# A one-core decoder layer: the lower-left block of the delta rule's inverse moves from the values to the scores

## The reference

```
def gated_delta_rule(q, k, v, g, beta):          # q, k, v: 32 x 128 x 8 heads x 128
    def step(S, inp):                            # S: heads x 128 x 128, one step per position
        qt, kt, vt, gt, bt = inp
        S = S * exp(gt)
        kv = einsum('bhk,bhkv->bhv', kt, S)
        delta = (vt - kv) * bt
        S = S + einsum('bhk,bhv->bhkv', kt, delta)
        return S, einsum('bhk,bhkv->bhv', qt, S)
```

## Time and profile before

| | before |
|---|---|
| median of three runs | 2331.67 us (2329.76 to 2333.71) |
| the profiled execution | 2329.89 us |
| its span, first to last instruction | 2327.9 us |
| PE busy | 2219.2 us (95%) |
| PE weight loads busy | 1901.7 us (82%) |
| DVE busy | 1678.1 us (72%) |
| ACT busy | 1404.4 us (60%) |
| POOL busy | 768.9 us (33%) |
| mean granted TensorE clock | 0.984 |

### The profile page before, as it was taken

How to read it: one execution, slowest core, us unless ns; L and a number is a source line. 1 busy time by engine, 2 the same in 40 slices (tenths; PEclk the granted TensorE clock), 3 DMA queues, 4 the chain that set the end, 5 groups by cost and what they waited for, 6 DMA issues and landing times.

```text
span 2327.9 us, 82936 instructions
## 1 busy us (share of the span) xinstructions
PE 2219.2 (95%) x33994; PEld 1901.7 (82%) x34026; DVE 1678.1 (72%) x5322; ACT 1404.4 (60%) x4326; POOL 768.9 (33%) x1771
## 2 busy tenths in 40 slices
PE   5899999999999999999999999999999999999986
PEld 4788888888888888888888888888888888888875
DVE  4577777777777777777777777777777777777753
ACT  3576555776555776555776555776555776555742
POOL 2332324333324332324332324333323333324321
PEclk8899999999999999999999999999999999999997
DMA  6000000000000000000000000000000000000000
GB/s 221 7 2 10 9 10 9 9 2 10 10 9 9 9 2 9 10 9 9 9 2 9 10 10 9 9 2 10 9 10 9 9 2 9 10 9 9 7 4 3
DMA packets 25065, 30.75 MB, mean 13 GB/s; under 512 B 8529, under 2 KB 21857, under 8 KB 23921
## 3 DMA queue, kind: packets, MB, share of 16 engines
q1 hardware_dynamic: 24688, 25.46, 3.3%
HBM read 21.25 MB, written 4.19 MB: 11 GB/s over the span
## 4 chain that ended last, share of the span: by engine, by line
PE 55%; DVE 22%; ACT 18%; issue 4%; POOL 1%; DVEq 0%; POOLq 0%
PE bank_b L644 10%; PE bank_a L460 6%; PE bank_b L736 5%; PE bank_b L652 5%; DVE acc L1010 4%; PE bank_a L542 4%; DVE diag L1046 3%; PE bank_b L673 3%; DVE y1p L1140 3%; DVE u L1087 3%; PE bank_a L581 3%; PE bank_a L572 3%; ACT prob L923 2%; ACT acc L814 2%; PE bank_a L532 2%
## 5 line engine op out<-in xcount | busy, mean ns | idle before, releaser
L1010 DVE SCALAR_TENSOR_TENSOR acc<-ypad,convw,acc 128x128 f32<-128x128 f32 x1536 | 432.2, 349 | 73.0 <-ACT acc L814 72.7
L460 PEld LDWEIGHTS bank_a<-xnT,wqkvz 128*128 128x128 f32 x2048 | 242.6, 195 | 43.3 <-DVE u L1087 42.8
L460 PE MATMUL bank_a<-xnT,wqkvz 128*128 128x128 f32 x2048 | 258.9, 281 | 17.1 <-DVE u L1087 17.1
L911 ACT ACTIVATE y1T<-bank_b 128x256 f32<-128x256 f32 x32 | 12.3, 384 | 313.0 <-PE bank_b L666 313.0
L1417 POOL TENSOR_SCALAR lnv<-mv 128x1 f32<-128x1 f32 x128 | 31.1, 243 | 509.5 <-DVE mv L1101 506.9
L923 ACT ACTIVATE prob<-bank_b,nmax 128x128 f32<-128x128 f32 x512 | 179.7, 374 | 2.2 <-DVE nmax L1160 1.8
L814 ACT ACTIVATE acc<-bank_a,convw 128x128 f32<-128x128 f32 x512 | 149.4, 405 | 0.0
L1321 POOL TENSOR_TENSOR gate<-ba,dtb 128x8 f32<-128x8 f32 x32 | 6.5, 203 | 430.3 <-ACT ba L825 430.3
L1158 DVE TENSOR_REDUCE smax<-bank_b 128x4 f32<-128x512 f32 x128 | 87.8, 686 | 68.5 <-PE bank_b L683 68.5
L736 PEld LDWEIGHTS bank_b<-y2T,wc 128*128 128x128 f32 x1024 | 124.3, 195 | 14.4 <-issue 14.4
L903 ACT ACTIVATE prob<-bank_b 128x512 f32<-128x512 f32 x64 | 38.2, 597 | 160.1 <-PE bank_b L644 160.1
(11 more groups left out here) (244 smaller groups left out, 5845.3 us busy)
## 6 DMA issues: line engine op xcount, KB each, us to landing
xin<-in_x_dram SPq DMA_DIRECT2D x32, 128.0 KB, 2.1
cin<-in_ctx_dram SPq DMA_DIRECT2D x32, 128.0 KB, 2.1
out_dram<-yout SPq DMA_DIRECT2D x32, 128.0 KB, 2.9
wqkvz<-in_wqkvz_dram SPq DMA_DIRECT2D x6, 512.0 KB, 6.8
wout<-in_wout_dram SPq DMA_DIRECT2D x1, 1024.0 KB, 9.8
wg<-in_wg_dram SPq DMA_DIRECT2D x1, 1024.0 KB, 11.4
wu<-in_wu_dram SPq DMA_DIRECT2D x1, 1024.0 KB, 13.4
wd<-in_wd_dram SPq DMA_DIRECT2D x1, 1024.0 KB, 15.2
```

The lines of the kernel that those rows point to most:

```text
L460: last = mm(A[bank][:, b * P:(b + 1) * P], wqkvz[:, c, o:o + P], xnT[:, c, :], start=(c == 0), stop=(c == KC - 1))
L1010: stt(acc[:, c, :], ypad[:, c, k:k + P], convw[:, c, k:k + 1], acc[:, c, :], ALU.mult, ALU.add).then_inc(conv.sem, 1)
```

## The change

`a_w0` and `a_w1` go, with their eight products and two subtractions. `a_mt` now has sixteen 64x64 products: eight for the lower-left block, written to the bottom half of `A[0]`, and eight more that apply the bottom 64-block to the bottom right of the scores, written to the bottom half of `A[3]`. They alternate between the top and the bottom rows of the array. ScalarE writes the first eight, negated, into the lower-left block of `zfull`; VectorE copies the other eight into the bottom right of `scoreT` (new step `a_low`). `a_sz0` and `a_sz1` now wait for both, and ScalarE copies the top half of their result alone, back into `scoreT`. `a_o` reads `scoreT` and the untouched values. The order lists of all four engines are new.

```diff
@@ TensorE
             def a_xT(n):
-                    pe.wait_ge(*w_ok(n - 1, 1))
+                    pe.wait_ge(*carry_ok(n - 1))
...
             def qkv(n, g):
-                    pe.wait_ge(*(w_ok(n - 1, 2) if g == 0 else core_ok(n - 1, 4 - g)))
+                    pe.wait_ge(*(lower_ok(n - 1) if g == 0 else core_ok(n - 1, 4 - g)))
...
             def a_mt(n):
+                pe.wait_ge(*score_ok(n))
                 pe.wait_ge(*zfull_ok(n)).then_inc(pe_passed.sem, 1)
                 for h in range(HV):
-                    last = mm(A[0][TOP, 64 * h:64 * h + 64], zfull[TOP, h, TOP], kkT[TOP, h, BOT], start=True, stop=True)
+                    part = slice(64 * h, 64 * h + 64)
+                    mm(A[0][BOT, part], kkT[TOP, h, BOT], zfull[TOP, h, TOP], start=True, stop=True)
+                    last = mm(A[3][BOT, part], zfull[BOT, h, BOT], scoreT[BOT, h, BOT], start=True, stop=True)
                 last.then_inc(carry_ps.sem, 1)
 
-            def solve_w(n, half):
-                pe.wait_ge(*carry_ok(n))
-                pe.wait_ge(*u_ok(n, 1 + half)).then_inc(pe_passed.sem, 1)
-                for b in range(4):
-                    h = 4 * half + b
-                    last = mm(A[(0, 3)[half]][BOT, b * P:(b + 1) * P], carryT[:, h, :], u[TOP, h, :], start=True, stop=True)
-                last.then_inc(w_ps.sem, 1)
-
             def score_z(n, half):
-                pe.wait_ge(*zfull_ok(n))
-                pe.wait_ge(*score_ok(n))
-                pe.wait_ge(*u_ok(n, 1 + half))
+                pe.wait_ge(*carry_ok(n))
+                pe.wait_ge(*lower_ok(n))
+                pe.wait_ge(*u_ok(n, 1 + half)).then_inc(pe_passed.sem, 1)
...
             def read(n, half):
-                pe.wait_ge(*sz_ok(n, 1 + half))
-                pe.wait_ge(*w_ok(n, 1 + half))
+                pe.wait_ge(*sz_ok(n, 1 + half)).then_inc(pe_passed.sem, 1)
-                    last = mm(A[1 + half][:, b * P:(b + 1) * P], szT[:, h, :], u[:, h, :], start=True, stop=True)
+                    last = mm(A[1 + half][:, b * P:(b + 1) * P], scoreT[:, h, :], u[:, h, :], start=True, stop=True)
@@ ScalarE
             def a_sq(n):
                 act.wait_ge(*mixed_ok(n, 2))
+                if not first(n):
+                    act.wait_ge(*o_ps(n - 1))
...
             def a_mt(n):
-                fn(carryT, A[0][TOP, :].rearrange("p (h c) -> p h c", c=64), ACT.Copy).then_inc(carry_ok.sem, 1)
+                fn(zfull[BOT, :, TOP], A[0][BOT, :].rearrange("p (h c) -> p h c", c=64), ACT.Copy, scale=-1.0).then_inc(carry_ok.sem, 1)
 
             def score_z(n, half):
-                fn(heads(szT, half), quad(A[1 + half]), ACT.Copy).then_inc(sz_ok.sem, 1)
+                fn(scoreT[TOP, 4 * half:4 * half + 4, :], quad(A[1 + half])[TOP, :, :], ACT.Copy).then_inc(sz_ok.sem, 1)
@@ VectorE
-            def solve_w(n, half):
-                dve.wait_ge(*w_ps(n, 1 + half))
-                tt(u[BOT, 4 * half:4 * half + 4, :], u[BOT, 4 * half:4 * half + 4, :], quad(A[(0, 3)[half]])[BOT, :, :],
-                   ALU.subtract).then_inc(w_ok.sem, 1)
+            def a_low(n):
+                dve.wait_ge(*carry_ps(n))
+                nc.vector.tensor_copy(scoreT[BOT, :, BOT], A[3][BOT, :].rearrange("p (h c) -> p h c", c=64)).then_inc(lower_ok.sem, 1)
@@ ORDER, one line of TensorE's list
-       "a_pa@1 a_vT1@1 a_pb@1 c_s a_mt@1 a_sz0@1 a_sz1@1 c_pT0 a_w0@1 a_w1@1 a_xT c_pT1 c_pT2 a_ba a_qkv0 "
+       "b_dn1@2 a_lb20@1 a_lb21@1 b_k@2 a_la30@1 a_la31@1 b_y1T@2 a_lb30@1 a_lb31@1 b_q@2 a_pa@1 a_pb@1 c_s "
```

More of the change, by code:

```diff
@@ L111 @@
 ORDER = dict(
[L112 removed]
[4 rows of a table removed]
[L117 to L122 removed]
[4 rows of a table removed]
[L127 to L129 removed]
+    pe="b_router@2 b_gu0@2 b_gu1@2 a_lb10@1 a_la11@1 b_gu2@2 b_gu3@2 a_lb11@1 b_dn0@2 a_la20@1 a_la21@1 "
[4 rows of a table added]
+       "a_la10".split(),
+    act="b_oT0@2 a_mix2@1 b_oT1@2 b_sum@2 b_cT@2 b_x2T@2 b_rl@2 a_sum a_mix3@1 b_sg0@2 b_sg1@2 b_rt@2 b_y1T@2 "
+       "a_zf@1 b_q@2 a_zo@1 c_exp0 a_mt@1 c_exp1 a_xT a_sz0@1 c_exp2 c_exp3 a_ba c_pT0 a_qkv0 c_pT1 a_o0@1 "
+       "a_sz1@1 c_R a_qkv1 a_o1@1 a_ln a_z0 a_mix0 a_seg a_mix1 a_z1 c_y2T a_sq c_h a_qkv2 a_st c_lt a_qkv3 "
+       "c_c0 c_te c_wT c_c1 a_dec0 a_dec1".split(),
+    dve="a_conv32@1 b_act0@2 b_act1@2 a_lb11@1 b_ys0@2 a_la20@1 a_la21@1 b_ys1@2 a_lb20@1 a_lb21@1 b_y1@2 "
[4 rows of a table added]
+       "a_lb10 a_la11".split(),
+    pool="c_y2b@3 c_ln2@3 b_mask@2 b_rs@2 b_xh@2 a_rq@1 a_xr@1 c_ln3@3 b_rd@2 a_x b_rt@2 b_ln0@2 a_ga b_y1b@2 "
+       "a_osc0@1 a_osc1@1 c_ln1 a_g c_rx c_sig a_sc".split(),
 )
@@ L780, in _ @@
                          c_lg=c_lg, c_wT=c_wT, c_spread=c_spread)
[L781 to L782 removed]
+            for name, f in (("a_z", zgate), ("a_vT", values), ("a_dec", exponents), ("a_sz", score_z), ("a_o", read), ("b_oT", core_T), ("b_w", project),
                             ("b_dn", down), ("c_c", columns), ("c_pj", mix)):
```

23 lines of the change are left out of this document (4 added, 19 removed), and 14 rows, old and new, of tables (dve, pe).

## The result

The changed kernel takes **2353.59 us** (median of four runs, 2348.28 to 2356.42), against 2331.96 before (2329.76 to 2333.71, four runs, of which the 2331.67 at the head of this document is the median of three): ratio 1.0098, 95% interval 1.0079 to 1.0116. It is 1% slower, where 2305 us was forecast and a faster kernel was given 0.80. The profiled execution took 2356.38 us, its span is 2354.6.

A forecast was written before the change was run, and what follows sets the result against it. PE, busy 95% of the span, was taken as the bound, with waits deciding the gain. Per trip -2.06 +0.50 +0.05 -0.40 +0.92 +0.20 = -0.79 us, over 32 sequences -25.3, giving 2305 us, range 2268 to 2330.

The forecast's parts named there:

- The rear part: From a_qkv2 to the next trip's first level product: same PE work; only leftover ScalarE delay reaches the next front part, +0.20.
- The granted clock and the gaps: Steady windows: clock read as 1.00 (2.4 GHz); one issue gap of 0.52 us noted as absent from most trips.
- Loading and the first and last trips keep their length: Start and end of the run: no change in time from loading or from the first and last trips.
- The middle part: From c_s to a_qkv2: stays at 20.2 us, as PE's waits grow from 0.49 to about 1.4, +0.92.
- `a_mt` overlaps: Lower-left block step: eight added products overlap the old eight fully, adding 0 of a possible 1.08 us.
- `a_pb` +0.50: Front part: without the value transpose covering VectorE's copy, the wait at a_pb grows from 0.16 to about 0.66 us.
- The table load waits for the core: ScalarE, rear part: load begins about 1.1 us before a_qkv2, takes 1.28; a_ss's input just ready in time.
- the slower rival: ScalarE's chain behind a_z0 holds PE at a_ss, then c_lg; loss of 19 us, 2349 us; chance 0.09.
- The front part: From the first level product to c_s: value transposes leave, 0.53 us each; wait terms +0.50, +0.05, fewer group entries -0.40.

The follow-up runs named there:

- e1: The changed kernel with a_conv22 and both c_gc steps moved ahead of c_weight on VectorE, so its taps no longer run beside GpSimd's products; 2332.22 us.
- e10: The changed kernel with the old kernel's rear-part order on PE, ScalarE and VectorE, its own order in front and middle; 2319.23 us, ratio 0.9954.
- e5: The changed kernel with level steps a_la20, a_la21, a_lb20, a_lb21 spread around b_dn0 and b_dn1 as before; 2348.82 us, ratio 1.0078.
- e13: e10 with the level steps spread around b_dn0 and b_dn1 as in the kernel before; 2317.83 us, ratio 0.9958.
- e4: The changed kernel's new arithmetic in the old order of steps, a_w taken out, a_low behind the second row maximum; 2358.91 us, ratio 1.014.
- e9: The kernel before with a_w0 and a_w1 left out and nothing in their place, so outputs lack the correction; 2330.83 us, ratio 1.0007.

## Why the prediction was wrong

- **The rear part, "The same PE work": this step failed.** It put the rear part's change at nothing, and it measured +1.41 a trip, 42 us over thirty trips. VectorE's work was not read beside GpSimd's. Taps were moved next to three products, and 1.13 us became 2.32, which PE saw as 0.83 at `b_oT0`. e1 takes 0.96 out of the rear part. Another 0.46 is left in e1 (21.49 against 21.03 in e10). In that part of e1 PE waits for nothing, so it is PE's own time: the same instructions take longer in the new order, by 0.07 to 0.12 in each of several steps (`a_kk` 0.99 for 0.89, `a_dec1` 0.95 for 0.86). The new list breaks up the groups of PE there, `a_ss`, `a_dec0`, `c_lg` and `a_st` standing between other steps, but what exactly of it costs 0.46 wasn't tried alone. Together 1.4 of the 1.41.
- **The granted clock and the gaps were taken as before.** The earlier trace rows show 1.00 in both windows, and the prediction used every duration at that level without asking what could change it. One issue gap of 0.52 was in the earlier trace rows and was set aside as rare. With the new list the gaps grow to 2.86 and the clock falls: 30.5 us above the shortest trips instead of 9.7. e5 and e13 show that the level steps' place decides most of it; e4 and e9 that waits do it too.
- **"Loading and the first and last trips keep their length" was wrong by 7.7 us** in the other direction: 5.2, 1.4 and 1.1, most of it before or in the first trip.
- **The middle part: right as a whole, wrong in its two terms.** It takes 20.40 where 20.21 was forecast, and `a_qkv2` waits 0.55 (forecast 0.5 to 0.9): the chain beside PE ends the part, as the prediction has it, and e9 shows the same (0.22 gained by 2.06 less work). But PE's waits in it grew from 0.49 to 0.96, not to 1.4, and PE's own time fell from 19.80 to 19.44, not to 18.8. The two errors of some 0.5 cancel because the chain decides. The transposes of the values take 0.59 and 0.65, not 0.53 each, and a group of four transposes that takes 0.44 in a stream of work (e9, 969.63 to 970.07) takes 0.66 behind a wait (`c_pT0` here, in e4 and in e10), so a wait costs PE more than its own length.
- **`a_mt` overlaps: right.** From its start to the next row are 1.08 us (1041.21 to 1042.29), for 32 instructions, as for sixteen before.
- **`a_pb` +0.50: right.** It starts 1.31 after `a_pa` and waits 0.62, where about 1.3 and 0.66 were forecast.
- **The table load waits for the core: right, and it just fits.** It starts at 1058.91, 1.0 before `a_qkv2`, and `a_ss` and `c_lg` follow no gap. So the slower rival, with its ScalarE chain at `a_ss`, did not occur. Its sign was right and its 2349 us lie near the result, but that is luck: the loss has another mechanism.

```profile
1058.91 1.28 ACT L811 ACT_TABLE_LOAD   x1 [0.95 <-DVE u L1078]
```

- **The front part: right, 27.49 forecast and 27.50 in e10.** In the changed kernel it is 27.12, as the late rear part leaves `x2` its time: `b_x2T` waits there in two trips alone, in e1 in 31, 0.32 in the quiet one. The single terms of this part weren't tried alone, so errors in them may cancel.

With the rear part as before, the forecast of a trip, 69.52 - 0.79 = 68.73, is 0.13 from e10's 68.86, and that is in the middle part. In the sum of the profiled executions, 2356.38 against 2304.6 is 51.8 us too much: 30 x 1.11 = 33.3 for the rear part, less what the front part gains by it (69.97 against 68.86), 30 x 0.13 = 3.9 for the rest of the trip, 20.8 above the shortest trips, 1.6 as the forecast takes its 0.79 for 32 trips and not for 30, less 7.7 at the ends, makes 51.9.

## What to carry to other kernels

Where a list is written anew, the part in which one engine does "the same work" must be read again for the other engines, each moved VectorE operation with two SBUF inputs beside what GpSimd does at that time. A busy share of 95% on PE says what PE does, not what its work is worth: e9 took 3% of it away for nothing, because another chain ended close behind. And a kernel that is so dense can lose more by short gaps than by the work that it saves: look at the issue gaps, at short waits that follow each other, and at the granted clock, trip by trip, since a mean of 0.99 over 700 us hid trips that were 2 to 6 us longer.
